# Gathering ten experts' tokens in quarter rows and turning them with VectorE instead of TensorE, in a mixture-of-experts kernel in fp32

## What is computed

```python
logits = jnp.einsum('bsd,de->bse', x, Wg) + bg
pv = jnp.transpose(jax.nn.softmax(logits, axis=-2), (0, 2, 1))
vals, idx = jax.lax.top_k(pv, 128)          # 128 tokens of each expert and batch
tok = x[bidx, idx]                          # [2, 16, 128, 512]
h = relu(einsum('bekd,edo->beko', tok, w1) + b1)
h = relu(einsum('bekd,edo->beko', h, w2) + b2)
h = einsum('bekd,edo->beko', h, w3) + b3
outputs = zeros.at[bidx, idx].add(h * vals[..., None])
```

## Time and profile before

| | |
|---|---|
| time, median of 3 runs (lowest to highest) | 744.17 us (743.77 to 746.02) |
| span of the profiled execution | 743.2 us |
| PE busy in the span | 716.2 us (96%) |
| PE's weight loads (PEld) | 624.9 us (84%) |
| DVE busy | 521.6 us (70%) |
| ACT busy | 401.9 us (54%) |
| POOL busy | 420.4 us (57%) |
| chain that ended last, share of the span | PE 84%, issue 6%, DMA 4%, DVE 3%, ACT 2%, POOL 1% |

### The profile page before, as it was taken

The page is one execution under the profiler, slowest core; times in us unless marked ns, Lnnn a source line. Parts: engine busy times, 40 slices in busy tenths (PEclk is TensorE's granted clock), DMA queues, the critical chain, the costliest instruction groups (busy, mean ns, idle before and its releaser), DMA issues.

```text
span 743.2 us, 12766 instructions
## 1 busy us (share of the span) xinstructions
PE 716.2 (96%) x4513; PEld 624.9 (84%) x4513; DVE 521.6 (70%) x978; ACT 401.9 (54%) x680; POOL 420.4 (57%) x621
## 2 busy tenths in 40 slices
PE   6999999999999999999999799999999999999994
PEld 5765888888888888888888778798999899899894
DVE  5786789889888888876896697464663565463561
ACT  5755444444544545868668334364664656464641
POOL 2825788888888887786788622503521443340132
PEclk9999999999999999999999899999999999999998
DMA  9610121221222213111117898696796698895534
GB/s 317 256 30 15 43 86 62 88 86 58 88 79 82 71 58 108 52 60 44 49 45 264 322 396 279 149 391 186 222 370 185 185 330 293 289 266 167 142 86 58
DMA packets 61671, 118.04 MB, mean 159 GB/s; under 512 B 6056, under 2 KB 7464, under 8 KB 61608
## 3 DMA queue, kind: packets, MB, share of 16 engines
q1 hardware_dynamic: 54312, 100.44, 38.7%
q0 software_dynamic: 7296, 16.78, 10.3%
HBM read 91.76 MB, written 25.21 MB: 157 GB/s over the span
## 4 chain that ended last, share of the span: by engine, by line
PE 84%; issue 6%; DMA 4%; DVE 3%; ACT 2%; POOL 1%; POOLq 0%; SPq 0%; DVEq 0%; ACTq 0%
PE bank L354 39%; PE banks L354 9%; PE bank L361 6%; PE bank L994 6%; PE banks L861 4%; PE banks L867 4%; DMA out<-y,ids 3%; PE banks L871 2%; PE banks L994 2%; PE banks L872 2%; PE banks L1423 1%; PE banks L1028 1%; PE bank L1318 1%; PE bank L1041 1%; DMA out<-x 1%
## 5 line engine op out<-in xcount | busy, mean ns | idle before, releaser
L2844 POOL DMA_INDIRECT out<-y,ids x24 | 46.1, 1922 | 157.4 <-DVE y L2555 155.5
L1973 DVE TENSOR_TENSOR w_l<-w_raw,w_h 128x2048 fp32r<-128x2048 f32 x35 | 80.1, 2291 | 63.2 <-ACT w_h L1496 49.4
L1961 DVE BATCH_NORM_STATS2 bn<-x 128x6 f32<-128x512 f32 x113 | 77.7, 688 | 8.2 <-DMA x<-x 5.4
L1496 ACT ACTIVATE w_h<-w_raw 128x2048 fp32r<-128x2048 f32 x36 | 68.5, 1918 | 7.2 <-DMA w_raw<-w 7.2
L1892 ACT ACTIVATE h<-bank,b 128x512 f32<-128x512 f32 x48 | 33.0, 688 | 62.5 <-PE bank L354 57.8
L1973 DVE TENSOR_TENSOR hT_l<-h,hT_h 128x512 fp32r<-128x512 f32 x48 | 33.0, 689 | 39.8 <-ACT hT_h L1898 37.7
L354 PE MATMUL bank<-tokT_h,w_h 128*128 128x256 f32 x188 | 55.1, 293 | 0.0
L2607 POOL TENSOR_SCALAR rstd<-mean_var 128x1 f32<-128x1 f32 x108 | 25.7, 238 | 50.9 <-DVE mean_var L1966 42.6
L354 PE MATMUL bank<-tokT_h,w_l 128*128 128x256 f32 x188 | 53.2, 283 | 0.0
L354 PE MATMUL bank<-tokT_l,w_h 128*128 128x256 f32 x188 | 53.2, 283 | 0.0
L354 PE MATMUL bank<-wf_h,xdT_h 128*128 128x512 f32 x128 | 52.6, 411 | 0.0
(11 more groups left out here) (419 smaller groups left out, 2380.1 us busy)
## 6 DMA issues: line engine op xcount, KB each, us to landing
w_raw<-w SPq DMA_DIRECT2D x36, 1024.0 KB
early_w<-w SPq DMA_DIRECT2D x24, 1024.0 KB, 10.0
x<-x SPq DMA_DIRECT2D x32, 256.0 KB, 2.7
out<-x SPq DMA_DIRECT2D x32, 256.0 KB, 2.0
xn<-xn SPq DMA_DIRECT2D x32, 256.0 KB
mask<-mask_t SPq DMA_DIRECT2D x8, 256.0 KB, 3.4
slot_all<-slots SPq DMA_DIRECT2D x4, 512.0 KB, 7.8
stage<-wk SPq DMA_DIRECT2D x1, 1024.0 KB, 7.7
```

The costliest lines, as they stand in the source:

```text
L1496: act.activation(dst, src, ACT.Copy).then_inc(sem, 1)
L1961: dve.bn_stats(bn6[which][:, j % 2, :], src[:, :]).then_inc(sem_bn[which], 1)
L1973: dve.tensor_tensor(dst, src, hi_part, ALU.subtract).then_inc(sem, 1)
L2844: pool.indirect_dma_start(out=out_rows, out_offset=bass.IndirectOffsetOnAxis(ap=ids[:, r:r + 1], axis=0), in_=y[e % 2][b][:, :], in_offset ...
```

## The change

Three things change together.

1. **The layout of the features.** The first-layer weights of all experts are loaded with `(p c) n` instead of `(c p) n`: partition p now holds the four features 4p to 4p + 3. So where TensorE still turns tokens, it reads every fourth column of a row (`of_chunk`): in 16 transposes of the early experts, 16 of e = 0 and 1, and 16 of the singles.
2. **The tokens of e = 2 to 11.** `gather_quarters` fetches each expert's rows with eight indirect DMAs of 128 quarter rows of 512 bytes, instead of two of 128 rows of 2 KB, with an index list `quarter_ids` that holds the token numbers repeated for four quarters. In that layout a transpose within 32x32 blocks is enough: VectorE's `turn_tokens` does it (two STREAM_TRANSPOSE of 128x512, reading at a step of four elements) and writes `tokT_raw` in SBUF; `turned_hi` and `turned_lo` make the rounded part and the rest from it, 128x1024 in one instruction each. TensorE's step `tokens(e)` is gone for these ten experts.
3. **The start of the stage and the singles.** ScalarE repeats the token numbers into `exps`, TensorE turns them with four transposes in place of two dummy matmuls, and VectorE adds the quarter number ahead of its copy of `vals`. `gather_single(1)` and `(2)` move from ahead of `add_single(0)` and `(1)` to behind the quarter gathers of e = 5 and e = 8.

```diff
+        def turn_blocks(eng, out, rows):
+            return eng.transpose(out.rearrange("p c (t k) -> p t c k", k=QBLK),
+                                 rows.rearrange("p (t k c) -> p t c k", t=P // QBLK, c=C))
+        def expert_weights(layer, e):
+            w = io.w[layer][e]
+            return w.rearrange("(p c) n -> p c n", c=C) if layer == 0 else chunked(w)
...
-        keep_warm(2, warm, ps_y[0])
+        pe.wait_ge(sm.a_rep, 1)
+        for t in range(C):
+            last = pe.transpose(ps[5][:, 2 * t * ROWS:2 * t * ROWS + HEADS], exps[0:HEADS, t * P:(t + 1) * P],
+                                ident[0:HEADS, 0:HEADS])
+        last.then_inc(sm.k_tq, 1)
...
-                    last = pe.transpose(bank[:, c * P:(c + 1) * P], tok[e % 2][:, b, c * P:(c + 1) * P], ident[:, :])
+                    last = pe.transpose(bank[:, c * P:(c + 1) * P], of_chunk(tok[e % 2][:, b, :], c), ident[:, :])
...
-            if e + 1 < JOINT:
+            if e + 1 < TURNED:
                 tokens(e + 1)
...
+        def turned_hi(e):
+            act.wait_ge(sm.d_tr, B * (e - 1))
+            hi(sm.a_thi, tok_h[:, :, :], tok_raw[:, :, :])
...
+        dve.wait_ge(sm.k_tq, 1)
+        dve.tensor_scalar(quarter_ids[:, :, :],
+                          ps[5][:, 0:2 * C * ROWS].rearrange("p (t r) -> p t r", t=C)[:, :, 0:HEADS:2],
+                          quarter[:, 0:1], None, ALU.add).then_inc(sm.k_quart, 1)
...
+        def turn_tokens(e):
+            dve.wait_ge(sm.p_h, 4 * e - 2)
+            for b in range(B):
+                dve.wait_ge(sem_tok[e % 2][b], tokens_in(e))
+                turn_blocks(dve, tok_raw[:, :, b * P:(b + 1) * P], tok[e % 2][:, b, :]).then_inc(sm.d_tr, 1)
+        def turned_lo(e):
+            dve.wait_ge(sm.a_thi, e + 4)
+            lo(sm.d_tlo, tok_l[:, :, :], tok_raw[:, :, :], tok_h[:, :, :])
...
+        def gather_quarters(e):
+            if e < 2 * TURNED:
+                pool.wait_ge(sm.p_tok, B * (e - 1))
+            else:
+                pool.wait_ge(sm.d_tr, B * (e - 3))
+            for b in range(B):
+                r = b * E + FIRST + e
+                for t in range(C):
+                    pool.indirect_dma_start(
+                        out=tok[e % 2][:, b, t * P:(t + 1) * P], out_offset=None, in_=xn4_quarters,
+                        in_offset=bass.IndirectOffsetOnAxis(ap=quarter_ids[:, t, r:r + 1], axis=0),
+                    ).then_inc(sem_tok[e % 2][b], 16)
...
+        pool.wait_ge(sm.k_quart, 1)
         for e in range(JOINT):
             if e + 2 < JOINT:
-                gather(e + 2)
+                gather_quarters(e + 2)
+            if SINGLE.get(e + 1, 0) > 0:
+                gather_single(SINGLE[e + 1])
             if e >= 1:
                 if e - 1 in SINGLE:
-                    if SINGLE[e - 1] + 1 < FIRST:
-                        gather_single(SINGLE[e - 1] + 1)
                     add_single(SINGLE[e - 1], e - 1)
                 add(e - 1)
```

More of the change, by code:

```diff
@@ L85, in build @@
         c_cut a_chain e_dve e_pe e_act e_pool e_logit
-        p_ev a_ev p_sv a_sv s_gather
+        p_ev a_ev p_sv a_sv s_gather d_tr a_rep k_tq k_quart
     """.split()
@@ L119, in build @@
     segbase = place("segbase", [P, 1])
+    quarter = place("quarter", [P, 1])
     bq = place("bq", [P, C])
@@ L288, in build @@
     assert top[0] <= at_xt1, (top[0], at_xt1)
+    quarter_ids = place("quarter_ids", [P, C, ROWS], U32, at=at_seg)
     tok_s = place("single_tok", [P, D], at=at_lists)
@@ L295, in build @@
     tok_h, tok_l = place("tokT_h", [P, C, B * P], F32R), place("tokT_l", [P, C, B * P], F32R)
+    tok_raw = place("tokT_raw", [P, C, B * P], at=at_qt + 4 * KB)
     tokT_s, h1_s = place("single_tokT", [P, D]), place("single_h1", [P, D])
@@ L362, in four_transposes, with of_chunk, four_row_transposes @@
         return last
+    def of_chunk(rows, c):
+        return rows[:, c::C]
+    def four_row_transposes(pe, bank, rows):
+        for c in range(C):
+            last = pe.transpose(bank[:, c * P:(c + 1) * P], of_chunk(rows, c), ident[:, :])
+        return last
+    def turn_blocks(eng, out, rows):
[4 more added lines that the diff above has]
+        return w.rearrange("(p c) n -> p c n", c=C) if layer == 0 else chunked(w)
     def blocks(t):
@@ L563, in token_bank, with tokens_in @@
         return ps_y[1] if (e, b) == (0, 1) and c >= 2 else ps_tok[b]
+    TURNED = 2
+    def tokens_in(e):
+        return 16 if e < TURNED else 16 + 64 * (e // 2)
     def used(eng, i):
@@ L623, in _ @@
         sp.dma_start(segbase[:, :], io.segbase).then_inc(sm.c_late, 16)
+        sp.dma_start(quarter[:, :], io.quarter).then_inc(sm.c_late, 16)
         for dst, src in ((b1, io.b1), (b2, io.b2), (b3, io.b3)):
@@ L987, in early_tokens @@
             pe.wait_ge(sem_tok_e[e], 16)
-            four_transposes(pe, bank, tok_e[e]).then_inc(sm.p_ev, 1)
+            four_row_transposes(pe, bank, tok_e[e][:, :]).then_inc(sm.p_ev, 1)
         def early_layer(bank, w, x, chunks):
@@ L1308, in tokens @@
             for b in range(B):
-                pe.wait_ge(sem_tok[e % 2][b], 16 * (e // 2 + 1))
+                pe.wait_ge(sem_tok[e % 2][b], 16)
                 if e == 0:
@@ L1325, in hidden @@
             if layer == 0:
-                pe.wait_ge(sm.d_tlo, 2 if e == 0 else B * (e + 1) + 1)
+                pe.wait_ge(sm.d_tlo, (2, 5)[e] if e < TURNED else e + 4)
                 xh, xl = tok_h, tok_l
@@ L1399, in single_tokens @@
             pe.wait_ge(sm.s_gather, 16 * (s + 1))
-            pe.wait_ge(sm.d_tlo, B * u + 3)
-            four_transposes(pe, ps_tok[1], tok_s).then_inc(sm.p_sv, 1)
+            pe.wait_ge(sm.d_tlo, 5)
+            four_row_transposes(pe, ps_tok[1], tok_s[:, :]).then_inc(sm.p_sv, 1)
         def single_first(s, u):
@@ L1876, in _ @@
         act.activation(ge[1][0:HEADS, :], top_v[:, :], ACT.Exp, bias=gmax[:, 1:2]).then_inc(sm.a_soft, 1)
+        act.wait_ge(sm.k_ids, 1)
+        act.activation(exps[0:HEADS, :].rearrange("p (t q k) -> p t q k", t=C, k=QBLK),
+                       top_i[:, :].rearrange("p (t k) -> p t k", k=QBLK).unsqueeze(2)
+                       .to_broadcast([HEADS, C, P // QBLK, QBLK]), ACT.Copy, scale=float(P // QBLK)).then_inc(sm.a_rep, 1)
         def token_hi(e):
@@ L1939, in _ @@
                     nxt += 1
+                if n == 0 and TURNED <= e + 1 < JOINT:
+                    turned_hi(e + 1)
                 if n == 0 and e in SINGLE:
@@ L2566, in _ @@
             hidden_lo(e, 0, 1)
-            if e + 1 < JOINT:
+            if e + 1 < TURNED:
                 token_lo(e + 1)
+            elif e + 1 < JOINT:
+                turn_tokens(e + 1)
             for n in range(2):
@@ L2574, in _ @@
                     weighted(e - 1, n)
+                if n == 0 and TURNED <= e + 1 < JOINT:
+                    turned_lo(e + 1)
             hidden_lo(e, 1, 0)
@@ L2900 @@
 CONSTS = 16 * 2
-LATE = 16 * 7
+LATE = 16 * 8
 def kernel(**inputs):
@@ L2925 @@
     arrays["later"] = -(p[:, None] > p[None, :]).astype(np.float32)
+    arrays["quarter"] = (p // 32).astype(np.float32).reshape(P, 1)
     arrays["segbase"] = (p // 64 * 2048 + p % 4 * 512).astype(np.float32).reshape(P, 1)
```

9 lines of the change are left out of this document (4 added, 5 removed).

## The result

| | before | with the change |
|---|---|---|
| time, median of 4 runs (lowest to highest) | 744.91 us (743.77 to 746.02) | 765.00 us (764.14 to 765.68) |
| span of the profiled execution | 743.2 us | 763.8 us |

The change makes the kernel slower: ratio 1.027, interval 1.0251 to 1.029. The forecast was 758 us, 735 to 768, slower with 0.59. The time went where the forecast had it, to PE's waits for the singles' tokens, but there is half as much again of it: 24.8 us, where it had 16.5.

What follows compares the result with a forecast made beforehand. PE, busy 96% of the span, was taken as the bound. -8.3 + 0.5 + 0.4 + 8.6 + 7.0 + 0.9 + 5.0 = +14.1 took the span from 743.2 to 757.3, forecast 758 us, range 735 to 768.

Steps and rivals of the forecast that it cites:

- PE's steps: Joint stage: taking the token-transposing step of ten experts off PE saves 7.9 to 8.7 us, taken as -8.3.
- The strided reads: 48 PE transposes loading rows at a step of 16 bytes cost 0.01 us each, +0.5 us; upper bound +6.7.
- The start: Start of the joint stage: id transposes replacing dummy matmuls and one more DVE instruction cost +0.4 us, between 0 and 0.8.
- VectorE: Joint stage: two transposes at 1.09 us each and a rest at 1.22 stay hidden ahead of PE, costing 0.
- The stalls: Joint stage: PE waits for late token rows of singles 1, 2 and 3, by 8.6, 7.0 and 0.9 us.
- POOL's pace: Joint stage: DVE's instructions hold POOL's indirect DMAs to 0.63 of their pace, 0.85 once PE stands.
- The landing of the single's addition: Before single 1: the second addition of e = 1 waits for that of single 0 to land, +3.4 us.
- The landing of the gather: At single 1: the rows are there 2.5 us after POOL has issued their gather.
- The backlog: Between singles 1 and 2: POOL has 45.2 us of work, does 39.2 in PE's 62.3; the other 6.0 take 7.0.
- A small stall: Rival, chance 0.08: POOL at 0.75 of its pace, first stall some 4 us, second none, 743 us.
- The clock: Behind two stalls PE's granted clock is at half, 2.5 us lost each time, +5.0 us.
- POOL keeps pace: Rival, chance 0.33: gathers delayed as little as earlier DMAs, a 1 us stall at single 1 only, 738 us.

## Why the prediction was right, and where its sizes were off

The forecast was slower, by POOL's lateness at the singles, and that is what the trace shows. 765 us lies in the range of 735 to 768, 7 us above the number. Step by step:

- **PE's steps.** Right: -8.4 in the joint stage, strided loads included, where the sum had -8.3 + 0.5.
- **The strided reads.** Right in the sum (0.011 us each, taken 0.01), by luck in its working: the loads themselves are half as long again, 209 ns against 141, and it is their overlap with the transposes that hides this. The Trainium skill (Advanced Engine Details and Errata, section Memory Cachelines) says that a read needs at least two hits on a line of 16 bytes, and names a penalty otherwise, without a figure; these loads agree with it. What was to show the term wrong, loads near 0.28 us, did not come.
- **The start.** +0.4 taken, +0.2 measured where the clock stayed full. The +1.8 of the profiled execution holds 1.6 of half clock, which no step had.
- **VectorE.** Right: the transpose was put at 1.09 us and took 1.086, the rest of 128x1024 at 1.22 and took 1.217, and PE waits for neither. Of the transpose only the total is borne out; no run parts it into the 0.69 and the 0.40 of the sum.
- **The stalls: "8.6", "7.0", "0.9".** POOL is late at the singles, as forecast; measured were 12.0, 12.2 and 0.6. *POOL's pace* was put at 0.63 while PE runs and 0.85 once PE stands. By the prediction's own prices POOL did 12 gathers and 4 additions, 22.9 us, from 514.00 to 551.49, when PE had come to stand. That took 37.5 us, 6.4 of them idle: a pace of 22.9 / 31.1 = 0.74. Behind that it did the other five gathers, 6.4 us, in 7.5: 0.85. So the first pace was too dear and the second right. *The landing of the single's addition* was worked out from one row as +3.4 and then left out of the sum of the stall, without a reason; POOL stood idle for it for 6.4 us. *The landing of the gather* was taken as 2.5 us, from the start of the stage, and was 4.5. With these three the first stall adds up: 29.3 - 0.74 x 35 leaves 3.4 us, which take 4.0; 6.1 for the landing of the addition (6.38 in place of the 0.30 between two issues) and 2.0 for that of the gather make 12.1. *The backlog* was wrong in kind at single 2: the sum carried POOL's lateness on, but POOL caught up, and waited at 590 us for `y`, which PE's stall had made late. From there it is the same 45.0 us again (590.68 to 635.66), so the second stall repeats the first.
- **The landings.** Both rows of before that the sum used are short. For the addition it is not that the DMA engines were less busy: their share was 1.01 from 515 to 520 us, where the 5.3 us come from, and 1.05 from 535 to 545 with the change (1.02 there before). What differs is whose packets ran, POOL's from 517 us on there and the weight loads' here, as shown above. The gather's 2.5 us come from a quieter place, from 470.9 to 473.5 us, where POOL's packets had 70% of the engines and no weight load ran.
- **The direction, in part luck.** With the measured pace of 0.74 and the rest of the sum as it stands, single 1 stalls for 4.0 us and single 2 not at all (0.74 x 62.3 = 46.1, of 45.2 us of work). That is the rival *A small stall*, 743 us, which had a chance of 0.08 and asked for a pace of 0.75. The sum came out slower because a pace that was too low stood in for a wait that had been left out.
- **The range.** The upper end of the forecast's own range adds up to 766.6 us from its terms, not 768; 765.0 lies below both.
- **The clock.** 2 x 2.5 taken, 2.5 + 1.8 measured.
- **The lock.** The Trainium skill (SBUF — State Buffer, section SBUF: two separate sides) has the one that starts first hold the other to its end. The runs agree for VectorE holding POOL: with the `w_l` cut to a sixteenth the gathers' mean falls from 1.248 to 1.074 us. They do not for the other way: 80 quarter gathers in place of 20 whole ones leave the mean of the `w_l` at 2.286 us, against 2.291.
- **The signs to look for.** The waits (6 to 10 and 4 to 9 us) were put too short, POOL busy "well above 80%" too high (73% in the first window, where it stood idle for 6.4 us for a landing and for 0.30 between any two issues), the gathers' mean of 1.5 too high (1.25).

The rival that POOL keeps pace (738) is what the kernel becomes with three gathers moved, and this version beats both: 735 us.

## What to carry to other kernels

On a queue that is served in order, the price of more small transfers is paid by whatever stands last behind them and is wanted soonest: here three DMAs of 256 KB in a stage of 290 us decide between 765 and 735. Before splitting transfers, list for each item behind them when it is wanted, and put those with the least slack first; the waits in the queue for landings count as work, at the landing times of a stretch in which other large loads run. And an off-path engine that issues DMAs must be timed with the holds of its neighbour, which the trace of before already shows in the instructions that are longer than their shortest.

## What was not expected of the hardware

- The landing of an indirect addition grew from 5.3 to 9.7 us, and of a gather from 2.5 to 4.5 and 6.2. The share of the DMA engines does not tell them apart (1.01 and 1.05 for the additions); the share of the weight loads in it does, 94.1% in the first three microseconds of the long addition.
- PE's granted clock fell to half at the start of the joint stage in some executions and not in others of the same instructions there: 0.50 in the changed kernel's and in that of the kernel with the singles first (470 to 472 us), 1.00 with the singles put back. What decides it is open; it costs 1.6 us in both.
- From the last addition's issue to the end of the span it takes 6.3 to 6.8 us in the eight kernels with quarter gathers and 8.0 to 8.5 in the three without, so some 1.2 to 2.2 us of every comparison with the kernel before come from there. Why is open.
